# Edge product of a graph layer with the two operands of the matmul exchanged and the messages turned back on PE

## The reference

```python
p1 = tanh(p @ pp_W1 + pp_b1) @ pp_W2 + pp_b2
inter = concat([p1[idx_i], p1[idx_j]]) @ pi_W1 + pi_b1
inter = (inter @ pi_W2 + pi_b2) @ pi_W3          # E x (64*8)
i1 = einsum('ecb,eb->ec', inter.reshape(E, 64, 8), basis)
i1 = tanh(i1 @ ii_W1 + ii_b1) @ ii_W2 + ii_b2
out = segment_sum(i1, idx_j)
```

## Time and profile before

| | |
|---|---|
| median of 3 runs | 6557.67 us |
| profiled execution, its own time | 6558.88 us |
| its span, first to last instruction | 6557.2 us |
| PE busy | 6130.7 us (93%) |
| DVE busy | 3046.6 us (46%) |
| ACT busy | 1896.5 us (29%) |
| POOL busy | 3798.3 us (58%) |
| edge stage in the trace | about 405 to 3150 us |
| counting part of it, sampled 1500 to 2000 us | PE 489.1, DVE 417.4, ACT 341.4, POOL 311.7 us busy |
| mean granted PE clock | 0.972 of 2.4 GHz |

### The profile page before, as it was taken

One profiled execution on the slowest core, in us unless ns is written; L12 is line 12 of the kernel. 1 busy time (PEld: TensorE's weight loads), 2 busy tenths in 40 slices (PEclk: granted clock), 3 DMA queues, 4 the chain that ended last, 5 costly groups with the idle time before them and its releaser, 6 DMA issues.

```text
span 6557.2 us, 137541 instructions
## 1 busy us (share of the span) xinstructions
PE 6130.7 (93%) x43472; PEld 4174.7 (64%) x43472; DVE 3046.6 (46%) x6105; ACT 1896.5 (29%) x3108; POOL 3798.3 (58%) x3700
## 2 busy tenths in 40 slices
PE   0779999999999999999689999999999999999998
PEld 0458888888888888888545555555555555555554
DVE  5478888888888888755431211222311111112101
ACT  1546666666666666411000000000000000000000
POOL 1156666666666666666056466566466567565664
PEclk9579999999999999999699999999999999999999
DMA  4233333333333333323378888888888888888886
GB/s 144 72 96 119 116 117 119 116 118 119 115 118 119 115 118 119 101 75 75 107 278 316 290 318 316 298 314 316 297 312 313 308 318 318 313 319 303 297 299 216
DMA packets 483676, 1353.66 MB, mean 206 GB/s; under 512 B 236756, under 2 KB 268052, under 8 KB 421399
## 3 DMA queue, kind: packets, MB, share of 16 engines
q1 hardware_dynamic: 275128, 1149.65, 47.9%
q0 software_dynamic: 118656, 176.66, 10.5%
q10 hardware_dynamic: 89538, 22.75, 1.7%
HBM read 1173.51 MB, written 175.21 MB: 206 GB/s over the span
## 4 chain that ended last, share of the span: by engine, by line
PE 49%; DVE 1%; issue 0%; ACT 0%; SPq 0%; DVEq 0%; DMA 0%; ACTq 0%
PE ps_a L1619 45%; PE ps_t L1661 1%; PE ps_t L1659 1%; PE ps_w L1581 1%; PE ps_t L1638 0%; PE ps_t L1663 0%; DVE to_window L1408 0%; PE ps_a L1571 0%; DVE sq L119 0%; DVE xc L1392 0%; DVE xc L107 0%; DVE sq L108 0%; DVE h L112 0%; DVE small L105 0%; DVE small L109 0%
## 5 line engine op out<-in xcount | busy, mean ns | idle before, releaser
L1619 PE MATMUL ps_a<-ring,table 128*128 128x448 fp8e4 (+1 forms) x15778 | 3060.1, 353 | 51.2 <-DVE table L120 34.8
L1276 POOL DMA_INDIRECT rows<-table_rows,gather_plan x2072 | 2000.8, 966 | 1382.0 <-issue 578.5
L690 POOL DMA_INDIRECT gathered<-u_source,plan x1576 | 1745.0, 1107 | 1186.3 <-issue 613.3
L1619 PEld LDWEIGHTS ps_a<-ring,table 128*128 128x128 f16 x15778 | 1512.0, 98 | 1390.8 <-issue 44.2
L730 ACT CAST unit<-ps_c 128x490 fp8e4<-128x490 f32 (+1 forms) x2080 | 1392.0, 669 | 737.3 <-PE ps_c L912 731.4
L977 PEld LDWEIGHTS ps_m<-M_sb,z 128*128 128x128 f32 x9408 | 1202.1, 192 | 95.2 <-issue 4.1
L977 PE MATMUL ps_m<-M_sb,z 128*128 128x64 f32 x9408 | 1181.8, 270 | 0.0
L1442 DVE TENSOR_TENSOR far_agg<-far_agg,ps_w 128x64 f32 x518 | 114.8, 222 | 2134.0 <-PE ps_w L1581 2120.4
L810 DVE TENSOR_TENSOR z<-ps_b,u 128x512 f32<-128x512 f32 x1184 | 801.6, 681 | 231.6 <-ACT u L719 200.0
L1312 ACT COPY agg<-ps_a 128x448 f32<-128x448 f32 (+1 forms) x161 | 85.3, 530 | 2771.7 <-PE ps_a L1619 2771.7
L912 PE MATMUL ps_c<-cell_hot,lane_hot 128*128 128x490 f16 x2080 | 744.0, 370 | 0.0
(11 more groups left out here) (235 smaller groups left out, 3490.7 us busy)
## 6 DMA issues: line engine op xcount, KB each, us to landing
ring<-counts SPq DMA_DIRECT2D x462, 1848.0 KB
counts<-unit SPq DMA_DIRECT2D x160, 792.0 KB, 3.9
dst_all<-dst_local SPq DMA_DIRECT2D x198, 256.0 KB
ring<-counts SPq DMA_DIRECT2D x21, 1584.0 KB
rows<-table_rows,gather_plan POOLq DMA_INDIRECT x2072
gathered<-u_source,plan POOLq DMA_INDIRECT x1576
table_rows<-table ACTq DMA_DIRECT2D x49, 448.0 KB, 3.9
window<-u_target SPq DMA_DIRECT2D x396, 32.0 KB
```

Source lines behind the costliest of these rows:

```text
L690: pool.indirect_dma_start(gathered[q][:, i, :, :].rearrange("p s d -> p (s d)"), None, Us, bass.IndirectOffsetOnAxis(ap=T["plan"][:, at:at ...
L1276: pool.indirect_dma_start(rows[:, s, t, :], None, G["tables"][n % 2], bass.IndirectOffsetOnAxis(ap=T["gather_plan"][:, at:at + 1], axis=0) ...
L1619: last = mm(ps_a[:, b, 0:width].rearrange("p (u c) -> p u c", c=UC), table[n % 2][:, k, :], cells, start=(k == 0), stop=(k == TILES - 1))
```

## The change

The product is turned round. M[k], 128 x 64, is the stationary side, and 512 columns of z (one half group) stream. Half group 0 goes to columns 0 to 63 of the array, so to partitions 0 to 63 of `ps_m`, and half group 1 to columns and partitions 64 to 127. `ps_m` then has features on the partitions and edges along them. The bias is one value per partition, a `bias` operand of the tanh; the bias matmul, its two operands and their set-up go. ACT writes the tanh to `msgT` (128 x 512). In the next step PE turns `msgT` back with four fp32 transposes into `ps_m`, and ACT copies that into `msg` (`take_msg`), with the tiles put in order. The orders change: on PE the turn comes after count 1, the two sums stand together after count 3, the product has two blocks (k = 0, 1 and k = 2, 3, in each k half 0 then half 1), with count 4, copy 4, count 5, copy 5 between them, and count 6, copy 6, count 7, copy 7, counts 8 to 12 after them. On ACT the order is take 0, empty 0, take 1, empty 1, take_msg, empty 2 to 5, tanh, empty 6 to 12. One more turn, copy and sum end the stage. The `general` form is changed likewise.

```diff
+            T["bias"] = esb("bias", [P, 1], F32)
+                     (T["bias"][0:D, :], w["ii_b1"].rearrange("o d -> d o")), (T["bias"][D:P, :], w["ii_b1"].rearrange("o d -> d o"))]
-            nc.vector.memset(T["bias_rows"][:, :, :], 0.0)
-            nc.vector.memset(T["bias_ones"][:, :], 0.0)
...
+        turned = ps_m[:, :].rearrange("p (j h d) -> p j h d", h=2, d=D)
+        rows_of = lambda q: msg[q][:, :, :].rearrange("p (h j) d -> p j h d", h=2)[:, :, :, 0:D]
...
+                def take_msg(t, q):
+                    act.wait_ge(S["turned"], 2 * t + q + 1)
+                    act.wait_ge(S["summed"], 2 * t + q)
+                    act.sem_inc(S["passed"], 1)
+                    nc.scalar.copy(rows_of(1 - q), turned).then_inc(S[f"msg{1 - q}"], 1)
...
+                        take_u(*following, 0)
+                        emptied([0])
+                        take_u(*following, 1)
+                        emptied([1])
+                        take_msg(t, q)
+                        emptied(range(2, 6))
                         act.wait_ge(S["m_done"], 4 + 4 * t + 2 * q + 2)
-                        nc.scalar.activation(msg[q][:, :, 0:D], ps_m[:, :, :], ACT.Tanh).then_inc(S[f"tanh{q}"], 1)
+                        nc.scalar.activation(msgT[:, :], ps_m[:, :], ACT.Tanh, bias=T["bias"][:, :]).then_inc(S["tanh"], 1)
+                        emptied(range(6, UB))
...
+                nc.vector.memset(msgT[:, :], 0.0)
...
+                def turn(before):
+                    pe.wait_ge(S["tanh"], before)
+                    pe.sem_inc(S["passed"], 1)
+                    for j in range(HT):
+                        last = nc.tensor.transpose(ps_m[:, j * P:(j + 1) * P], msgT[:, j * P:(j + 1) * P], T["ident"][:, :])
+                    last.then_inc(S["turned"], 1)
...
+                        turn(g)
+                        for h in range(2):
+                            copy_basis(*following, 2 + h)
+                            counted([2 + h])
                         for h in range(2):
                             sum_half(1 - q, t + q, g, h)
-                            copy_basis(*following, 2 + h)
-                            counted([2 + h])
-                        pe.wait_ge(S[f"tanh{1 - q}"], t + q)
+                        pe.wait_ge(S[f"msg{1 - q}"], t + 1)
+                        pe.wait_ge(S["z_done"], 16 * t + 8 * q + 24)
                         pe.sem_inc(S["passed"], 1)
-                        mm(ps_m[:, :, :].rearrange("p t d -> p (t d)"), T["bias_ones"][:, :], T["bias_rows"][:, :, :].rearrange("p t d -> p (t d)"), start=True, stop=False)
-                        for i in range(ET):
...
-                            for k in range(4):
-                                last = mm(ps_m[:, i, :], z[2 * q + h][:, k, i % HT * P:(i % HT + 1) * P], T["M"][:, k, :], start=False, stop=(i == ET - 1 and k == 3))
-                            if i % HT == HT - 1:
-                                last.then_inc(S["m_done"], 1)
-                            counted([4 + i])
-                            if i < 4:
-                                copy_basis(*following, 4 + i)
-                        counted([UB - 1])
+                        for k in range(4):
+                            for h in range(2):
+                                last = mm(ps_m[D * h:D * h + D, :], T["M"][:, k, :], z[2 * q + h][:, k, :], start=(k == 0), stop=(k == 3))
+                                if k == 3:
+                                    last.then_inc(S["m_done"], 1)
+                            if k == 1:
+                                for i in range(2):
+                                    counted([4 + i])
+                                    copy_basis(*following, 4 + i)
+                        for i in range(2):
+                            counted([6 + i])
+                            copy_basis(*following, 6 + i)
+                        counted(range(8, UB))
...
+                turn(EGROUPS)
```

More of the change, by code:

```diff
@@ L572, in edges @@
         msg = two(sb, "msg", [P, ET, D + 1], F32)
+        msgT = sb("msgT", [P, EH], F32)
         lane_hot = two(sb, "lane_hot", [P, UB, P], F16)
@@ L590, in edges @@
         hot = [t[:, :, :].rearrange("p b e -> p (b e)")[:, 0:GC] for t in z[0:2]]
+        turned = ps_m[:, :].rearrange("p (j h d) -> p j h d", h=2, d=D)
+        rows_of = lambda q: msg[q][:, :, :].rearrange("p (h j) d -> p j h d", h=2)[:, :, :, 0:D]
         banks = [t[:, :] for t in (*ps_u, *ps_b)]
-        V = {n: sem("v_" + n) for n in "dve basis ends rows u u_out copied z m tanh stored back placed hot used taken".split()}
+        V = {n: sem("v_" + n) for n in "dve basis ends rows u u_out copied z m tanh turned msg stored back placed hot used taken".split()}
         blk = c.enter_context(nc.Block())
@@ L751, in regular @@
                     step(t, False)
+                take_msg(STEPS, 0)
             def general(act):
@@ L759, in general @@
                     act.wait_ge(V["m"], 2 * g + 2)
+                    nc.scalar.activation(msgT[:, :], ps_m[:, :], ACT.Tanh, bias=T["bias"][:, :]).then_inc(V["tanh"], 1)
+                    act.wait_ge(V["turned"], g + 1)
                     act.wait_ge(V["stored"], 16 * g)
                     act.sem_inc(S["passed"], 1)
-                    nc.scalar.activation(msg[0][:, :, 0:D], ps_m[:, :, :], ACT.Tanh).then_inc(V["tanh"], 1)
+                    nc.scalar.copy(rows_of(0), turned).then_inc(V["msg"], 1)
             choose(act, regular, general)
@@ L916, in sum_half @@
                     if h == 0:
-                        pe.wait_ge(S[f"tanh{q}"], n)
+                        pe.wait_ge(S[f"msg{q}"], n + q)
                         pe.wait_ge(S[f"to{q}"], n)
@@ L1014, in general @@
                         pe.sem_inc(S["passed"], 1)
-                        for i in range(4):
-                            for k in range(4):
-                                last = mm(ps_m[:, HT * h + i, :], z[h][:, k, i * P:(i + 1) * P], T["M"][:, k, :], start=False, stop=(h == 1 and i == HT - 1 and k == 3))
+                        for k in range(4):
+                            last = mm(ps_m[D * h:D * h + D, :], T["M"][:, k, :], z[h][:, k, :], start=(k == 0), stop=(k == 3))
                         last.then_inc(V["m"], 1)
-                pe.wait_ge(V["tanh"], EGROUPS)
+                    pe.wait_ge(V["tanh"], g + 1)
+                    pe.sem_inc(S["passed"], 1)
+                    for j in range(HT):
+                        last = nc.tensor.transpose(ps_m[:, j * P:(j + 1) * P], msgT[:, j * P:(j + 1) * P], T["ident"][:, :])
+                    last.then_inc(V["turned"], 1)
+                pe.wait_ge(V["msg"], EGROUPS)
                 def add_up(n, first=False, final=False):
```

37 lines of the change are left out of this document (8 added, 29 removed).

## The result

The changed kernel takes 6800.04 us (median of four runs, 6794.92 to 6804.96), the kernel before 6556.75 us in the same job (four runs, 6555.32 to 6566.88): ratio 1.0366, 95% interval 1.0351 to 1.0382. It is slower by 3.7%; the forecast was 6772 us.

A forecast was written before the change was run, and what follows sets the result against it. PE was taken as the full engine, DVE next at 83%. The profiled 6559 us plus 187 (counting groups), 25 (groups without counting) and 1 (other edits) gave 6772 us, about +3.2%, range 6480 to 7300 us (82%).

The forecast's parts named there:

- wrong above all if the blocks come out under 1.9 us: Sign against the forecast: blocks of the product with M, expected at about 2.45 us, measuring under 1.9 us.
- the forecast mechanism: Late basis copies behind product blocks delay DVE, making a closed PE-DVE round of 15.66 us per counting group; 56%.
- The stream: Product with M on PE: each fp32 record of 512 columns takes 0.43 us, sixteen in a row 6.9 us.
- A change of shape each way: Around each product block PE goes from 128 to 64 columns and back: 0.3 us for both ways.
- The overlap: Column halves overlap partly, in program order: five record times per block, 2.15 us, or 2.45 us with shape changes.
- R: Closed round through PE and DVE, with basis copies late behind product blocks: 15.66 us a counting group, 12.53 without counting.
- P: PE's own round, with counts 8 to 12 at ACT's pace: 12.8 us plus up to 2, not the longest.
- Rival 4: The clock falls: half of the stage at 1.2 GHz, 725 us more, 7497 us; 5%.
- Groups without counts: The 36 edge-stage groups without counting work: 12.53 us each against 11.83 before, +25 us in all.
- The turn: Four fp32 transposes on PE, 0.44 us a group, covered by the wait for DVE's first product; uncovered, 86 us.
- Full overlap of the halves: Rival: halves interleave record by record, shape change hidden, 1.72 us a block, 6486 us; 9%.
- DVE's own beat: Rival: basis copies are not late, so DVE sets the beat at 13.2 us a counting group, 6325 us; 11%.

The follow-up runs named there:

- the mended order: Changed kernel with copies 4, 5 and counts 4 to 6 before the first block, ACT unloadings 2 to 11 before the tanh, `from_node` after product 3: 6395.63 us.
- the filler run: Changed kernel with an unused 384-column matmul on PE after each of counts 8 to 12: 6728.74 us.

## Why the prediction was right and wrong

The time was right, 6772 against 6800 us, and so was the sign; but that they are only 28 us apart is luck, what is left of larger errors that offset each other. The forecast had +187 and +25 us for the two kinds of group, measured are +143 and +95. By its own sign ("wrong above all if the blocks come out under 1.9 us") the forecast mechanism was wrong.

- *The stream.* 0.43 us a record: measured 0.427 (1500.67 to 1501.10). A change of shape each way, 0.3 together: 1.88 less 4 x 0.427 leaves 0.17 for the way back, and the copy ahead of a block takes 0.31 us (1502.69 to 1503.00) instead of 0.21, 0.10 for the way in. Together 0.27.
- *The overlap, the step that failed.* I let the second record of a half hold back all behind it and so counted five record times to a block, 2.45 us. It takes four, 1.88 us, in either order of the code. In two blocks that is 1.14 us a group too much. The Trainium skill, "TensorE: Matmul & The Clock Gate", section The mechanism (Part 3), says that matmuls start and end strictly in program order; the run with the order of the halves changed disagrees, 0.02 us between the starts of the first and the fifth record in that order. "TensorEngine Tiling (Array Packing)", section Theoretical Speedup, has up to twofold; the trace agrees, eight records in the time of four.
- *Which round is the longest, the second step that failed.* With 1.88 in its terms R is 15.66 - 1.14 = 14.5 us, and DVE would hardly have been late. I had put P at 12.8 us "plus up to 2" and below R. With the measured blocks it starts at 7.46 + 0.44 + 3.75 + 0.2 (the way in, twice) = 11.85 us. In the group shown the tail, from copy 7's 0.21 (1505.51 + 0.21) to the join (1509.96), is 4.24 us where five counts in a stream take 1.05; in the next group, which has no wait before the join, it is 3.9. That is 2.85 us on top, not up to 2: 14.7 us, and the shorter groups measure 14.7. To the waits that I had in mind come the counts that no longer overlap, 0.43 us each, and the slow unloadings 6 and 9, each with 0.77 us to the next one instead of 0.48. Every second group has 0.4 us more by the wait before the join and 0.9 by the clock. The run with copies early (no gain) shows that it is not R, and the one with counts early that R would bind only at 17.6 us with those counts in it. In the mended order one count less in the tail takes another 0.55 us off the group.
- *The clock.* Rival 4 had half the stage at 1.2 GHz, 5%. It came in a smaller dose: 0.44 us a counting group on average, some 70 us in all by the filler run. In the groups without counts, sums and first block take 1.76 us more than at the full clock, some 60 us.
- *Groups without counts, the third step that failed.* 12.53 us forecast, 14.55 measured. The round had no window in it, and no slow clock. With blocks of 1.88 its own sum would be 11.4 us. In the order before, the load was early enough (two waits for it, 1.3 us together, from 2850 to 3140); with the copies after the product, m7, and SP's load that follows it, move to the end of the group, and `from_node` waits 1.4 us for it in front of product 1. Moving it gives 11.37, by 2.0 us of wait and work and 1.3 of clock.
- *The small terms.* The turn is 0.44 as forecast, but not covered: with P the longest, it stands on the path. The tanh was to keep its 0.60 and measures 0.69: "ScalarE: Activation LUTs" of the Trainium skill, section What ACT_TABLE_LOAD costs, puts a bias read through a pointer at 93 ns more, and the trace has 88 (599 to 687 ns). Start and end together were -2.4 us, forecast +1 with bounds of -2 and +3; the start varies by more than that from run to run.
- *The rivals.* Full overlap of the halves (9%) was true, though the change of shape was not hidden; the time it would have given did not come, because another round was behind it at once. DVE's own beat (11%) was out of reach of this order and is reached by another.

So the change holds what it promises on PE, 3.2 us a group, and the orders that came with it take 4.1 us. With the same product and other orders, `from_node` late among them, the kernel is 4.0% faster than before.

## What to carry to other kernels

Work out every closed round that runs through the moved instructions, each engine's own among them, and put its tail at what the slower partner gives (unloads of ACT, two banks), not at the streamed price of its instructions. When a product comes in long blocks, place ahead of it whatever others wait for and behind it only what is already free to go; one count moved took 0.55 us off each of 160 groups, some 87 us. And when an engine gets shorter by a new order, look at each queue whose trigger (here m7) has moved towards the end of the group.

## What the runs showed of the hardware

- Two fp32 matmuls of 128x64 by 512 columns on the two column halves run fully at once, 0.427 us a pair of records, and the later one in the program is not held back by an earlier one that waits for its own half. On one half, and on the same PSUM partitions, the same eight records take 3.58 us instead of 1.87.
- PE fell to 1.2 GHz for the 3 us of the join after four waits of 0.4 to 0.8 us in 4.2 us (1505.72 to 1509.96). In the next group, with three waits (0.79, 0.38, 0.51) and none before the join, the granted clock was 1.00 through the join (1525 to 1530). It was 1.00 in the filler run too (1506 to 1510), where the four waits are 0.79, 0.21, 0.35 and 0.27. In the run with the old product it was 0.50 for 14 us without any wait (3608 to 3622).
- A count that has to wait keeps PE for 0.37 to 0.43 us besides the wait, in a stream it adds 0.21. Waits so small are paid twice.
- ACT's unloading of 128x490 from PSUM to fp8, 98 pieces of five bytes 64 bytes apart, takes about 0.6 us at nine of thirteen offsets, 0.49 for the last, smaller one, and 0.77 to 1.01 us where the five bytes reach over a multiple of 16 (unloadings 3, 6 and 9), in every group of before and after.
- Changing from matmuls of 128 columns to 64 and back costs 0.10 and 0.17 us, and a turn of 128x512 by four fp32 transposes 0.44 us.
